# A graph and expert layer on one core: half of a weight subtraction goes to GpSimd, results are read back block by block, and a table is made in five pieces

## The reference, cut to what matters

```
logits = tokens @ router_w.T
rw, re = top_k(softmax(logits), 2);  rw = rw / rw.sum(-1)
combine = zeros(N, 8); combine[row, re] = rw
out = tokens
for e in range(8):
    h = gelu(tokens @ w1[e] + b1[e])          # 256 -> 256
    out = out + combine[:, e] * (h @ w2[e] + b2[e])
x = x + out
```

## Time and profile before

| | |
|---|---|
| median of three runs | 684.38 us (683.26 to 685.10) |
| profiled execution | 681.67 us, its span 679.8 us |
| PE busy | 563.5 us (83%), 4972 matmuls |
| DVE busy | 486.1 us (72%) |
| ACT busy | 340.8 us (50%) |
| POOL busy | 134.9 us (20%) |
| granted PE clock, whole span | 0.922 of full speed |
| chain that ended last | PE 67%, DVE 14%, DMA 7%, ACT 4%, issue 4% |

### The profile page before, as it was taken

How to read it: one execution, slowest core, us unless ns; L and a number is a source line. 1 busy time by engine, 2 the same in 40 slices (tenths; PEclk the granted TensorE clock), 3 DMA queues, 4 the chain that set the end, 5 groups by cost and what they waited for, 6 DMA issues and landing times.

```text
span 679.8 us, 13374 instructions
## 1 busy us (share of the span) xinstructions
PE 563.5 (83%) x4972; PEld 500.2 (74%) x4972; DVE 486.1 (72%) x1091; ACT 340.8 (50%) x597; POOL 134.9 (20%) x132
## 2 busy tenths in 40 slices
PE   0769975487999999999999999999857969998550
PEld 0235442366999999998889999999846969898540
DVE  5792899736999999997648564376588675856195
ACT  0023865439777778774021001235365868888330
POOL 2000000000000000000000000006856687656160
PEclk9967999579999999999999999999966989999595
DMA  7999999999755522500007876524626536457546
GB/s 182 210 197 192 194 198 197 194 198 195 278 213 243 238 124 124 242 2 1 1 1 273 330 330 277 234 73 139 207 77 209 162 113 195 144 158 216 141 122 222
DMA packets 80301, 119.83 MB, mean 176 GB/s; under 512 B 8718, under 2 KB 68915, under 8 KB 78574
## 3 DMA queue, kind: packets, MB, share of 16 engines
q1 hardware_dynamic: 70766, 105.91, 58.8%
q0 software_dynamic: 9472, 13.07, 6.0%
HBM read 49.74 MB, written 71.15 MB: 178 GB/s over the span
## 4 chain that ended last, share of the span: by engine, by line
PE 67%; DVE 14%; DMA 7%; ACT 4%; issue 4%; POOL 1%; SPq 1%; ACTq 0%; DVEq 0%; POOLq 0%
PE psB L1487 24%; PE psC L1487 5%; PE psB L1688 5%; PE psA L1402 4%; PE psD L1402 4%; PE psC L1390 4%; PE psC L1715 3%; DMA acc<-in_x_dram 3%; DMA xs<-expert_slots 2%; DVE hot L766 2%; PE psA L1670 2%; PE psD L1549 2%; PE psD L1715 1%; PE psD L1500 1%; DVE stats L703 1%
## 5 line engine op out<-in xcount | busy, mean ns | idle before, releaser
L1487 PE MATMUL psB<-hs,counts 125*128 125x256 f16 x1600 | 209.5, 273 | 0.0
L1487 PEld LDWEIGHTS psB<-hs,counts 125*128 125x128 f16 x1600 | 171.8, 140 | 0.4 <-DVE part L941 0.2
L766 DVE TENSOR_TENSOR hot<-iota_j,places 128x2048 bf16<-128x2048 bf16 x128 | 154.3, 1222 | 15.5 <-PE psA L1402 9.7
L637 POOL IOTA row_of<- 128x25 f32 x1 | 0.2, 237 | 411.1 <-DVE acc L816 411.1
L648 POOL DMA_INDIRECT expert_slots<-rows,place x50 | 61.3, 1226 | 68.2 <-issue 54.6
L1746 ACT CAST counts<-psA 128x1000 f16<-128x1000 f32 x64 | 63.5, 993 | 20.5 <-PE psA L1402 19.9
L1746 ACT CAST counts<-psD 128x1000 f16<-128x1000 f32 x64 | 63.5, 993 | 17.1 <-PE psD L1402 17.1
L1688 PE MATMUL psB<-xT_hi,w_now 128*128 128x256 f32 x256 | 51.3, 304 | 10.3 <-issue 10.3
L1402 PE MATMUL psA<-hot 128*128 128x125 bf16 x512 | 49.6, 220 | 8.0 <-DVE hot L766 3.2
L1804 ACT ACTIVATE part<-psB 128x256 f16<-128x256 f32 x32 | 12.4, 386 | 85.4 <-PE psB L1487 85.4
L1487 PE MATMUL psC<-hs,counts 125*128 125x256 f16 x400 | 52.8, 273 | 0.0
(11 more groups left out here) (328 smaller groups left out, 989.7 us busy)
## 6 DMA issues: line engine op xcount, KB each, us to landing
expert_slots<-zeros SPq DMA_DIRECT2D x8, 3432.0 KB, 43.5
kept_counts<-counts SPq DMA_DIRECT2D x6, 4000.0 KB, 12.3
counts<-kept_counts SPq DMA_DIRECT2D x6, 4000.0 KB, 12.4
xs<-expert_slots SPq DMA_DIRECT2D x32, 264.0 KB, 3.1
back<-expert_out SPq DMA_DIRECT2D x10, 560.0 KB
w_raw<-in_L_ffn_w_dram SPq DMA_DIRECT2D x2, 2048.0 KB, 9.7
acc<-in_x_dram SPq DMA_DIRECT2D x1, 2800.0 KB
out_dram<-acc SPq DMA_DIRECT2D x5, 560.0 KB
```

The costliest lines, as they stand in the source:

```text
L766: v.tensor_tensor(hot[:, slot].rearrange("p g w n s -> p (g w) n s"), iota_j[:, :, :].unsqueeze(1).to_broadcast([P, 2 * pairs, P, PAIR]), ...
L1487: m = pe.matmul(sum_bank(g, d), counts5[0:PT, buf, a, d, :], hs2[0:PT, a, :, :].rearrange("p q f -> p (q f)"), start=first, stop=last, ski ...
```

## The change

Four edits:

1. `w2_low` on DVE forms the low parts of experts 0 to 3 only. POOL forms those of experts 4 to 7 with the same subtraction, after `spread_block(2)` and in front of `spread_block(3)`, once ACT has the high parts. The semaphore of the low parts becomes two, one for w1 and one for w2; ACT's first copy of w1 waits for both halves of w1.
2. `load_back(0)` goes in front of tile 29's load and `load_back(1)` in front of tile 31's; `load_back(2)` and `load_back(3)` follow the last tile's load, then store(0), store(1), load_back(4) and the other stores.
3. Four `final_add` in the loop run after tiles 27 to 30 instead of 28 to 31.
4. `table(s)` is cut into `table_levels`, `table_ends`, `table_past`, `table_rows` and `table_experts`. Rows come ahead of experts and have a semaphore of their own, for which SP waits. Stages 0 and 1 call the five in a row; for stage 2 they run after tiles 4, 5, 6, 7 and 8.

```diff
-        BACK_FROM = 29
+        BACK_FROM = (29, 31)
...
-                    sp.wait_ge(table_ok, 2 * s + 2)
+                    sp.wait_ge(rows_table_ok, s + 1)
                     sp.wait_ge(spread[s], 16 * 2 * W * (STAGE_BLOCKS[s] if s == 0 else 1))
-                if n == BACK_FROM:
-                    for c in range(BACKS):
-                        load_back(c)
+                if n in BACK_FROM:
+                    load_back(BACK_FROM.index(n))
...
+            load_back(2)
+            load_back(3)
             store(0)
-            load_back(3)
             store(1)
             load_back(4)
...
-            for c in range(C - 1):
+            for c in range(C - 2):
                 spread_block(c)
+            pool.wait_ge(w_hi_ok, 3)
+            half = slice(EXPERTS // 2, EXPERTS)
+            pool.tensor_tensor(w2_lo[:, half], w2_raw[:, half], w2_hi[:, half].bitcast(F32), ALU.subtract).then_inc(w2_lo_ok, 1)
+            spread_block(C - 2)
...
-        FINAL_FROM = MOE_TILES - 2 * (BACKS - 1)
+        FINAL_FROM = MOE_TILES - 2 * (BACKS - 1) - 1
...
+            def table_past(s):
+
+                quota, levels = STAGE_AT[s + 1] - STAGE_AT[s], s + 1
+                pe_, pn_ = past_of(s)
+                st.wait()
+                st.did(v.tensor_tensor(pe_, run_end..., ident_row..., ALU.is_le))
+                st.wait()
+                st.did(v.tensor_tensor(pn_, pe_, run_step..., ALU.mult))
+
+            def table_rows(s):
...
+                st.did(v.tensor_reduce(tn_, pn_, AX.X, ALU.add))
+                st.wait()
+                st.did(v.scalar_tensor_tensor(tn_, ident_row[0:1, 0:quota], float(SLOT), tn_, ALU.mult, ALU.add))
+                st.wait()
+                v.tensor_scalar(tab_r[...], tn_, run_at..., float(EXPERTS * REGION), ALU.add, ALU.min).then_inc(rows_table_ok, 1)
+
+            def table_experts(s):
...
+                if s:
+                    st.did(v.tensor_tensor(pn_, pe_, expert_step..., ALU.mult))
+                    st.wait()
                 st.did(v.tensor_reduce(te_, pn_ if s else pe_, AX.X, ALU.add))
...
             def w2_low():
 
                 v.wait_ge(w_hi_ok, 3)
-                v.tensor_tensor(w2_lo, w2_raw, w2_hi.bitcast(F32), ALU.subtract).then_inc(w_lo_ok, 1)
+                half = slice(0, EXPERTS // 2)
+                v.tensor_tensor(w2_lo[:, half], w2_raw[:, half], w2_hi[:, half].bitcast(F32), ALU.subtract).then_inc(w2_lo_ok, 1)
...
+                if t == 4:
+                    table_levels(2)
+                if t == 5:
+                    table_ends(2)
                 if t == 6:
-                    table(2)
-                if t >= FINAL_FROM:
+                    table_past(2)
+                if t == 7:
+                    table_rows(2)
+                if t == 8:
+                    table_experts(2)
+                if FINAL_FROM <= t < MOE_TILES - 1:
                     final_add((t - FINAL_FROM) // 2, (t - FINAL_FROM) % 2)
...
-                        act.wait_ge(w_lo_ok, 1)
+                        act.wait_ge(w1_lo_ok, 2)
```

More of the change, by code:

```diff
@@ L412, in gps_layer @@
         table_ok = sem("table_ok")
+        rows_table_ok = sem("rows_table_ok")
         spread = [sem(f"spread{s}") for s in range(STAGES)]
@@ L1139, in total_read, with runs_of, past_of, table_levels @@
                 v.tensor_scalar(parts[:, s], total_of(s), 1.0 / SLOT, None, ALU.mult).then_inc(total_used, 1)
[L1141 to L1151, removed]
+            def runs_of(s):
+                return slice(LEVELS - EXPERTS * (s + 1), LEVELS)
+            def past_of(s):
+                return past_e[:, 0:STAGE_AT[s + 1] - STAGE_AT[s], runs_of(s)], past_n[:, 0:STAGE_AT[s + 1] - STAGE_AT[s], runs_of(s)]
+            def table_levels(s):
                 v.wait_ge(total_used, s + 1)
@@ L1168, in table, with table_ends @@
                 st.wait()
-                st.did(v.tensor_tensor(len_, to, frm, ALU.subtract))
+                st.did(v.tensor_tensor(length[:, 0:s + 1], level[:, 1:s + 2], level[:, 0:s + 1], ALU.subtract))
+            def table_ends(s):
+                levels, wide = s + 1, [1, s + 1, EXPERTS, EXPERTS]
+                to, len_, end_, taken_ = level[:, 1:s + 2], length[:, 0:levels], run_end[:, 0:levels], taken[:, 0:levels]
                 st.wait()
@@ L1178, in table @@
                 st.wait()
-                st.did(v.tensor_tensor(pe_, end_.rearrange("p k e -> p (k e)").unsqueeze(1).to_broadcast([1, quota, EXPERTS * levels]),
+                at = run_at[:, runs_of(s)].rearrange("p (k e) -> p k e", e=EXPERTS)
+                st.did(v.tensor_tensor(at, to, end_, ALU.subtract))
+                if s < STAGES - 1:
+                    st.did(v.tensor_tensor(taken_, len_, end_, ALU.subtract))
+                st.wait()
+                st.did(v.scalar_tensor_tensor(at, at, float(SLOT), region_at[0:1, :].unsqueeze(1).to_broadcast([1, levels, EXPERTS]), ALU.mult, ALU.add))
@@ new lines, in table_ends @@
+                if s < STAGES - 1:
+                    st.did(v.tensor_scalar(taken_, taken_, float(STAGE_AT[s + 1] - STAGE_AT[s]), 0.0, ALU.add, ALU.max))
+                st.wait()
+                following = slice(LEVELS - EXPERTS * levels + 1, LEVELS + 1)
+                st.did(v.tensor_tensor(run_step[:, runs_of(s)], run_at[:, following], run_at[:, runs_of(s)], ALU.subtract))
+            def table_past(s):
+                quota, levels = STAGE_AT[s + 1] - STAGE_AT[s], s + 1
+                pe_, pn_ = past_of(s)
+                st.wait()
+                st.did(v.tensor_tensor(pe_, run_end[:, 0:levels].rearrange("p k e -> p (k e)").unsqueeze(1).to_broadcast([1, quota, EXPERTS * levels]),
@@ L1186, in table @@
[L1186 to L1195, removed]
+                st.did(v.tensor_tensor(pn_, pe_, run_step[:, runs_of(s)].unsqueeze(1).to_broadcast([1, quota, EXPERTS * levels]), ALU.mult))
+            def table_rows(s):
+                quota, first = STAGE_AT[s + 1] - STAGE_AT[s], LEVELS - EXPERTS * (s + 1)
+                pe_, pn_ = past_of(s)
+                tn_ = tile_n[:, 0:quota]
@@ L1200, in table @@
                 st.wait()
-                first = LEVELS - EXPERTS * levels
-                v.tensor_scalar(tab_r[:, now], tn_, run_at[:, first:first + 1], float(EXPERTS * REGION), ALU.add, ALU.min).then_inc(table_ok, 1)
+                v.tensor_scalar(tab_r[:, STAGE_AT[s]:STAGE_AT[s + 1]], tn_, run_at[:, first:first + 1], float(EXPERTS * REGION),
+                                ALU.add, ALU.min).then_inc(rows_table_ok, 1)
+            def table_experts(s):
+                quota, levels = STAGE_AT[s + 1] - STAGE_AT[s], s + 1
+                te_ = tile_e[:, 0:quota]
+                pe_, pn_ = past_of(s)
+                if s:
+                    st.did(v.tensor_tensor(pn_, pe_, expert_step[:, runs_of(s)].unsqueeze(1).to_broadcast([1, quota, EXPERTS * levels]), ALU.mult))
+                    st.wait()
+                st.did(v.tensor_reduce(te_, pn_ if s else pe_, AX.X, ALU.add))
+                if s < STAGES - 1:
+                    st.did(v.tensor_tensor(taken[:, 0:levels], taken[:, 0:levels], length[:, 0:levels], ALU.min))
+                st.wait()
+                v.tensor_scalar(tab_e[:, STAGE_AT[s]:STAGE_AT[s + 1]], te_, EXPERTS - 1.0, None, ALU.min).then_inc(table_ok, 1)
                 if s < STAGES - 1:
@@ L1206, in table @@
                         st.wait()
+            def table(s):
+                table_levels(s)
+                table_ends(s)
+                table_past(s)
+                table_rows(s)
+                table_experts(s)
             def w1_low(half):
@@ L1211, in w1_low @@
                 v.wait_ge(w_hi_ok, half + 1)
-                v.tensor_tensor(w1_split[:, 0, part], w1_raw[:, part], w1_split[:, 1, part].bitcast(F32), ALU.subtract).then_inc(w_lo_ok, 1)
+                v.tensor_tensor(w1_split[:, 0, part], w1_raw[:, part], w1_split[:, 1, part].bitcast(F32), ALU.subtract).then_inc(w1_lo_ok, 1)
             def w2_low():
                 v.wait_ge(w_hi_ok, 3)
-                v.tensor_tensor(w2_lo, w2_raw, w2_hi.bitcast(F32), ALU.subtract).then_inc(w_lo_ok, 1)
+                half = slice(0, EXPERTS // 2)
+                v.tensor_tensor(w2_lo[:, half], w2_raw[:, half], w2_hi[:, half].bitcast(F32), ALU.subtract).then_inc(w2_lo_ok, 1)
             def rest(i, g):
@@ L1299, in _ @@
                     if t in STAGE_AT:
-                        v.wait_ge(table_ok, 2 * stage + 2)
+                        v.wait_ge(table_ok, stage + 1)
                     e = v.value_load(tab_e[0:1, t:t + 1], min_val=0, max_val=EXPERTS - 1)
```

12 lines of the change are left out of this document (4 added, 8 removed).

## The result

| | before | after |
|---|---|---|
| median (range) | 683.82 us (683.18 to 685.10), 4 runs | 667.49 us (665.34 to 669.91), 4 runs |
| ratio, 95% interval | | 0.976 (0.9722 to 0.9798) |
| profiled execution, its span | 681.67, 679.8 | 667.08, 665.2 |
| DVE busy / POOL busy | 486.1 / 134.9 | 487.8 / 136.9 |
| granted PE clock, whole span | 0.922 | 0.933 |

A forecast was written before the change was run, and what follows sets the result against it. It took tile 29's transfer stall, the third table and the second weights' subtraction on DVE as the bounds; 12.6 + 5.8 - 1.4 = 17.0 us off 684.38 gave 667.4 us, range 662.0 to 672.5.

The forecast's parts named there:

- 0.9 us are to spare: Read-back: tile 29's load lands at 625.1, PE frees itself near 626, so the stall there goes.
- the zero for tile 31: Read-back: tile 31's load lands at 634, PE wants it about 633, but DVE sets the pace; costed at nothing.
- Rival C: Transfer stall moves instead of going: tile 31 or 29 lands 3 us after DVE's cover ends; 670.4 us, chance 0.11.
- I keep 22.4: End of kernel, y(31) through last scatter, block 4's load, additions and store: stays 22.4 us as before.
- 1 us either way: End of kernel: the last scatter could meet less traffic or more, changing the time by 1 us.
- the new bound: Tile 12's load needs block 4's rows in place, so tile 12 starts at 561.7 instead of 567.56, 5.8 us less.
- the piece of 1.9 us fit just so: Third table's ends piece fits DVE's idle ahead of h_lo; costed at nothing, 0.4 us if one sticks out.
- rival A: Second weights: the ports don't matter, DVE isn't held, the chain gains 2.14 - 0.2; 664.1 us, chance 0.22.
- shift should just slip ahead: DVE's shift at 505.36 runs before GpSimd's subtraction holds DVE; gap is held instead, starting 3.4 us late.
- rival B's shift case: GpSimd's subtraction already stops shift, before gap: 1.5 us more than forecast, 668.9 us; rival B's chance 0.12.
- leave the chain: Second weights: DVE giving up half its 4.33 us subtraction ahead of block 4's count takes 2.14 us off the chain.
- The 0.2 us for table 1: Reordered table 1, on the chain: fewer operations overlap, but one stretched operation may not be; costs 0.2 us.

The follow-up runs named there:

- one_block_no_gpsimd: Kernel after with DVE forming all second weights' low parts, only block 0 read back in the loop, ahead of tile 30, others behind tile 31: 662.36 us, ratio 0.9686.
- gpsimd_alone: Kernel before with only the second weights' edit, GpSimd subtracting half of the low parts: 686.26 us, ratio 1.005.
- table_alone: Kernel before with only the table edits (rows ahead of experts, third table in five pieces): 675.86 us, ratio 0.9901.
- store1_later: Kernel before with store(1) issued behind load_back(4) instead of ahead of it: 683.12 us, ratio 0.9986.
- load3_late: Kernel after with DVE forming all second weights' low parts and block 3's load behind store(0) and store(1): 669.04 us, ratio 0.9791.
- spread_early: Kernel after with DVE forming all second weights' low parts and block 4's scatters at t = 2 instead of 3: 663.75 us, ratio 0.9704.
- writes_only: Kernel after with GpSimd filling zeros instead of subtracting, that half's low parts left out: 665.89 us in a single run.

## Why the prediction was right

The time was 0.1 us from the forecast, and that is partly luck: its terms were off by up to 2.4 us and cancelled, and the gain of 17.0 us was taken off a median of before of 684.38, which now stands at 683.82. Several of the signs named beforehand came out beside their marks: PE's wait ahead of tile 29 (1.07 us for "under 1"), the landings at tiles 29 and 31 (6.6 for "under 6", 10.4 for "8 to 10"), y(26) to y(31) (19.0 for "about 17.5"), the wait ahead of tile 12 (0.50 for "1 to 2"), and y(31) to the end (20.0 for "21 to 23").

**Read-back.** The mechanism was right: the stall went, the clock kept 1.00, and DVE's additions set the pace of the last tiles. Its size was not: 11.1 us instead of 12.6. The step that failed is "0.9 us are to spare" for tile 29 and the zero for tile 31. Tile 29's load went out at 619.41, close to my 619.9, but landed 6.6 us later, at 626.0 instead of 625.1, and PE was ready at 625.0 instead of 626. At tile 31 PE waited another 1.68. I had worked out when the bytes ahead of the load would be through to a tenth of a microsecond and set it against a PE time known no better. one_block_no_gpsimd shows both steps: with no wait for a load the stretch is 17.12 us, against 17.5 forecast and 19.03 in after. Rival C was thus half true: the stall moved in part, 2.8 us of waiting, of which 1.9 show in the stretch.

**The end.** The step "I keep 22.4" failed, by 2.4 us in favour. I had the block loads' order before me and called its effect on the last scatter "1 us either way". The scatter lands 3.11 us sooner than before, and block 4's load takes 0.76 longer (7.06 for 6.30). The 3.11 have two parts. The first, 1.88 us, is the scatter's own time on GpSimd: 2.86 us in the old order (before, gpsimd_alone, table_alone, store1_later), 0.97 or 0.98 in every kernel that reads the blocks back one by one. Its cause stays open. It isn't store(1), nor load 3 by itself, nor that DVE is adding beside it: the additions begin 2.02 us ahead of the scatter in both kernels (658.06 and 660.08, 645.84 and 647.86). The second, 1.2 us, lies between that and the landing. Before, block 3's load was issued at 655.20, 4.9 us ahead of the scatter, and store(1) at 660.14 beside it; in after, the load went out at 637.41 and the store 1.2 us and more ahead. load3_late shows that such a load can do it: issued 1.6 us ahead of the scatter, it stretches the landing from 2.76 to 7.36 us. How much of the 1.2 is the load and how much the store isn't shown.

**The third table.** 5.99 against 5.8, with the new bound as named. (The forecast's own terms, 557.6 + 0.8 + 3.1, give 561.5 and not 561.7, so a gain of 6.1.) The stretch was made differently inside: the forecast waits 1.5 us for tile 12, the trace only 0.50. PE was late itself, because the pieces are not free. After two of them DVE starts its next to_row late (timeline of DVE, after):

```profile
551.58 0.17 DVE L1346 TENSOR_SCALAR to_row<-xs 128x2 int32 x1 [0.62 <-issue]
...
556.07 0.17 DVE L1346 TENSOR_SCALAR to_row<-xs 128x2 int32 x1 [0.66 <-issue]
```

With the two gaps y(4) to y(6) takes 8.4 us, against 7.6 before. The forecast let "the piece of 1.9 us fit just so" at no cost, 0.4 if one stuck out. The trace names no releaser for the two gaps ("issue"), 0.62 and 0.66 us, and no run tried what makes them. They cost nothing in the end, since block 4's rows set the time anyway, as spread_early bears out from the other side.

**The second weights.** The mechanism was right, and rival A, that DVE isn't held, is refuted by the traces of after and gpsimd_alone: GpSimd's subtraction holds DVE's two-input operation for its length, 4.73 and 4.72 us for 0.17, where beside the fills of writes_only such operations keep their 0.15 to 0.17. Of the other direction the traces show one scatter that takes 2.36 us for 1.19 while DVE subtracts for 2.28 (before, after, gpsimd_alone and writes_only); "keeps GpSimd from reading" is my inference from that, and no run shows what the scatter waits for. The subtraction took 4.50 us; I had taken 4.9.

The mis-sized step is where the hold falls. I had "shift should just slip ahead" and gap held, with 1.51 us of other DVE work done under GpSimd's subtraction. Counted from block 4's statistics, my start of 505.33 is 4.82 us in (500.51 in the profile of before); the trace has 4.24, and 4.20 in gpsimd_alone. The last scatter ended 0.3 us sooner against DVE, the subtraction followed it after 0.03 us instead of the 0.30 between scatters, and the hold took in a step of DVE that had begun 0.2 us ahead of it. So DVE was caught in its inverse square root, where every step that is left is a two-input operation and waits for the one before, and none of the 1.51 us was done. The held step lost 4.73 - 0.17 = 4.56 us; less the 2.14 saved that is the 2.42 in the table. It is like rival B's shift case, but four steps earlier on DVE than shift, with the shorter subtraction.

The 2.14 us that "leave the chain" are the other weak term. They are there at the token transposes, but in writes_only, where nothing is held, only 0.3 us of them is left at y(0). So no run shows rival A's gain of 1.9 us, even for a GpSimd that didn't hold DVE. The 0.2 us for table 1 didn't show either: its stretch is 15.66 us in both kernels.

**Where the chances stood.** Faster was all but certain and came. The two terms that made it so were each shown alone. The forecast's loss on the GpSimd edit had the right sign; leaving the edit out would have been worth more than the forecast gave it, 2.7 us for 1.2.

## What to carry to other kernels

Work on an idle engine was not free here: GpSimd's subtraction held a two-input operation of DVE, the critical engine, for 4.73 us where it takes 0.17, and GpSimd's fills held none. For such a subtraction I would put a hold of its full length into the sum, from the first two-input operation after its start, and compare that with what it takes off; for other work, look in a trace whether it holds anything. Follow what it takes off to the next point where all paths meet: 2.2 us gained at one point were 0.3 at the next in writes_only. Look for bulk transfers ahead of the small ones that somebody waits for: three blocks ahead of tile 29's load cost PE 11.1 us, one ahead of tile 29's and one ahead of tile 31's cost it 1.07 and 1.68, and block 3 ahead of the last scatter stretched its landing from 2.76 to 7.36 us. Where time to spare comes out under 1 us by such a sum, as the 0.9 at tile 29, take the order that needs none: with one block, ahead of tile 30, PE had no wait at tiles 29 to 31. A total that comes out right says little: cut both traces at common points and hold every term against its own.

## What the runs showed of the hardware

- GpSimd's subtraction of 128 x 2048 fp32 with fp32r output takes 4.50 us (after, gpsimd_alone), DVE's 2.28 (after). DVE's held step, 4.73 and 4.72 us for 0.17, begins 0.20 and 0.19 us ahead of GpSimd's listed start (507.23 and 507.43, 506.26 and 506.45) and ends 0.03 us after its end.
- GpSimd's fills of 128 x 1536 and 128 x 2048 fp32 take 1.40 and 1.82 us, and DVE's two-input steps of 125 x 5 beside them took 0.15 to 0.17 us (writes_only).
- An indirect write of 128 rows lands after 2.8 us where the DMA engines moved 40 GB/s beside it (after), and after 7.4 with a 1.28 MB read issued 1.6 us ahead of it (load3_late).
- In after a tile's load behind one block's read-back landed 6.6 us after its issue, and one behind two blocks after 10.4 us; the rate was 232 to 271 GB/s.
- PE's 20 products of 128 x 125 by 128 x 8 fp32 take 2.25 us at a granted clock of 1.00 (before) and 4.21 us at 0.50 (writes_only).
